# Relation passes of a graph network: three accumulators in turn in place of one

## The reference

```python
t = jnp.einsum('nd,rdo->rno', h, weight)
msg = t[etype, src]
agg = jax.ops.segment_sum(msg, dst, num_segments=h.shape[0])
return jax.nn.relu(agg + bias)
```

## Time and profile before

| | us |
|---|---|
| Median of 3 runs | 8612.98 |
| Lowest and highest of them | 8594.42, 8615.65 |
| Profiled execution: span from its first to its last instruction | 8619.9 |
| Busy in the span: POOL, PE, PEld, DVE, ACT | 5243.4, 4852.2, 2990.1, 3573.0, 1730.7 |
| Pass 1, from 4014 us on | about 1200 |
| Pass 3, from 7417 us on | about 1167 |

### The profile page before, as it was taken

One profiled execution on the slowest core, in us unless ns is written; L12 is line 12 of the kernel. 1 busy time (PEld: TensorE's weight loads), 2 busy tenths in 40 slices (PEclk: granted clock), 3 DMA queues, 4 the chain that ended last, 5 costly groups with the idle time before them and its releaser, 6 DMA issues. The chain is left out here.

```text
span 8619.9 us, 69117 instructions
## 1 busy us (share of the span) xinstructions
PE 4852.2 (56%) x17004; PEld 2990.1 (35%) x17004; DVE 3573.0 (41%) x9196; ACT 1730.7 (20%) x7055; POOL 5243.4 (61%) x5610
## 2 busy tenths in 40 slices
PE   3202235555557777777455543777777876655554
PEld 1100014444435555543333332222223663333332
DVE  4201014333335555564222224444445776244445
ACT  0000001111123333322000002222223874000000
POOL 5577756666666666632666662666665882366665
PEclk6655557777778888888666666878888998866666
DMA  3001012222235555554333335656666884333333
GB/s 96 2 3 39 15 40 90 90 89 89 91 116 176 177 175 175 177 114 156 92 93 93 92 93 67 186 184 187 187 187 177 267 271 156 117 93 92 91 94 85
DMA packets 422550, 1037.69 MB, mean 120 GB/s; under 512 B 159993, under 2 KB 188189, under 8 KB 415516
## 3 DMA queue, kind: packets, MB, share of 16 engines
q0 software_dynamic: 223616, 552.46, 22.9%
q1 hardware_dynamic: 198556, 480.95, 17.4%
HBM read 716.74 MB, written 316.30 MB: 120 GB/s over the span
## 5 line engine op out<-in xcount | busy, mean ns | idle before, releaser
L944 POOL DMA_INDIRECT rel_rows<-relation_rows,rel_ring_row x1640 | 1558.3, 950 | 1177.7 <-ACT rel_ring_end L937 695.1
L956 PE MATMUL rel_sums<-rel_rows,rel_hot 128*128 128x256 f32 x3280 | 1197.1, 509 | 1178.3 <-issue 448.5
L956 PEld LDWEIGHTS rel_sums<-rel_rows,rel_hot 128*128 128x128 f32 x3280 | 785.7, 252 | 1590.1 <-issue 1076.9
L982 DVE TENSOR_TENSOR g_acc<-rel_sums,g_acc 128x256 f32 x1224 | 517.8, 423 | 1532.9 <-DMA records_by_dst<-g_big 548.5
L1913 POOL DMA_INDIRECT nmax_rows<-messages,nmax_ring_row x832 | 788.6, 948 | 566.3 <-ACT nmax_ring_row L1869 327.6
L761 POOL DMA_INDIRECT rows_by_src<-spread_rows,spread_ring_place x832 | 803.2, 965 | 483.8 <-issue 254.3
L838 POOL DMA_INDIRECT both_rows<-batch_normed,both_ring_row x832 | 791.0, 951 | 460.9 <-ACT both_ring_end L807 231.3
L605 POOL DMA_INDIRECT records_by_dst<-sort_ring_rec,sort_ring_place x784 | 810.4, 1034 | 390.6 <-issue 241.2
L739 PE MATMUL spread_p_r<-g_big,spread_hot_t 128*128 x1664 | 631.5, 545 | 542.0 <-ACT spread_hot_t L674 358.8
L1961 DVE TENSOR_TENSOR g_big<-nmax_short,g_big 128x512 f32 x832 | 575.7, 692 | 659.9 <-PE nmax_short L1934 288.6
L1934 PE MATMUL nmax_short<-nmax_rows,g_ident_b 128*128 128x512 bf16 x2496 | 800.3, 436 | 0.0
(11 more groups left out here) (443 smaller groups left out, 6114.8 us busy)
## 6 DMA issues: line engine op xcount, KB each, us to landing
kept_rows<-nmax_rows SPq DMA_DIRECT2D x208, 536.0 KB
g_big<-kept_rows SPq DMA_DIRECT2D x208, 536.0 KB
both_out_rows<-rows_by_src SPq DMA_DIRECT2D x202, 520.0 KB
att_local_row<-local_of_edge SPq DMA_DIRECT2D x52, 512.0 KB
rel_rows<-relation_rows,rel_ring_row POOLq DMA_INDIRECT x1640
relation_rows<-mix_table SPq DMA_DIRECT2D x25, 1024.0 KB
relation_rows<-fin_table SPq DMA_DIRECT2D x25, 1024.0 KB, 3.9
rows_by_src<-spread_rows,spread_ring_place POOLq DMA_INDIRECT x832
```

The source lines that it names most:

```text
L944: pool.indirect_dma_start(rows[:, j, 0:words], None, table, bass.IndirectOffsetOnAxis(ap=ring_row[:, j:j + 1], axis=0)).then_inc(landed[n ...
L956: last = nc.tensor.matmul(sums[:, unit % slots, 0:width], hot[:, j, :], rows[:, j, :], start=of == 0, stop=of == GRAIN[k] - 1)
L982: nc.vector.tensor_tensor(at, sums[:, unit % slots, 0:width], at, ALU.add).then_inc(added, 1)
```

## The change

The sums go in turn to three accumulators: unit 0 to `acc`, unit 1 and 2 to two accumulators in `g.big`, unit 3 to `acc` again. An add waits for the add three back, the last one that wrote the same accumulator. ScalarE clears the two new ones, after it has staged the first eight groups; the second and third sum wait for that (`blank`). After the last sum, VectorE adds both into `acc`.

```diff
@@ aggregate
         sums = m.ps("sums", [P, slots, 8 * 512 // slots])
+        side = g.big[:, 0:2 * (T + 1) * width].rearrange("p (a t d) -> p a t d", a=2, d=width)
+        into = [acc[:, :, 0:width], side[:, 0], side[:, 1]]
+        blank, joined = m.sem("blank"), m.sem("joined")
@@ scalar
             for n in range(groups):
+                if n == ring:
+                    for s in range(2):
+                        nc.scalar.activation(side[:, s], g.iota[:, 0:1].unsqueeze(2).broadcast_to([P, T + 1, width]),
+                                             ACT.Copy, scale=0.0).then_inc(blank, 1)
                 if n >= ring:
                     act.wait_ge(summed, n - ring + 1)
@@ vector
-                    if unit:
-                        dve.wait_ge(added, unit)
-                    at = acc[:, bass.ds(tiles[unit % 16], 1), 0:width].rearrange("p t d -> p (t d)")
+                    if unit in (1, 2):
+                        dve.wait_ge(blank, unit)
+                    if unit >= 3:
+                        dve.wait_ge(added, unit - 2)
+                    at = into[unit % 3][:, bass.ds(tiles[unit % 16], 1), :].rearrange("p t d -> p (t d)")
                     nc.vector.tensor_tensor(at, sums[:, unit % slots, 0:width], at, ALU.add).then_inc(added, 1)
             dve.wait_ge(added, groups * per)
+            for s in range(2):
+                if s:
+                    dve.wait_ge(joined, 1)
+                nc.vector.tensor_tensor(into[0], into[0], side[:, s], ALU.add).then_inc(joined, 1)
+            dve.wait_ge(joined, 2)
```

## The result

| | before | changed |
|---|---|---|
| Median of 9 runs, us | 8607.44 | 8632.24 |
| Lowest and highest, us | 8594.42, 8615.65 | 8626.14, 8643.96 |
| Span of the profiled execution, us | 8619.9 | 8630.4 |

The changed kernel takes 1.0033 times as long, with a 95% interval of 1.0025 to 1.0042: slower by 28 us, or by 24.8 us if one goes by the medians. It lies at the bound of 0.3% that the prediction drew between no change and slower.

The account below looks back on a forecast made before the run. The prediction took GpSimd's gathers, one per 1.25 us plus stalls from late counts, to bound the two passes. From a median of 8612.98 us, joins +28.6, body -3 and tail -5 gave 8633 us, range 8598 to 8655.

Parts of the forecast that it names:

- the case with no credit: Rival, chance 0.30: late counts let the faster adds win nothing in body or tail; the joins stand alone, 8642 us.
- The 8 us of credits: Savings expected in pass 3 from the loosened waits: 3 us in the body and 5 us in the tail.
- Joins, +28.6: Two VectorE adds of 128x6656 after each pass's last sum, nothing beside them: 14.3 us per pass, 28.6 for both.
- Zeroing, 0: ScalarE's clearing of the two new accumulators, 5.7 us each, hidden behind VectorE's wait for the first gather: 0 us, 1 at most.
- Adds 0.34 us apart: VectorE's adds, waiting for the add three back, would start 0.34 us apart instead of 0.567.
- Body, -3: During pass 3, quicker adds might let TensorE get a group further before the next slow stretch: 3 us saved.
- The comparison of pass 1 with pass 3: Stalls per group, 0.69 us with two adds and 0.74 with four, taken to cap the body's gain at 10 us.
- a sign of being right: TensorE's waits for adds in pass 3 would be well under 408 us, with hardly any time won.
- Tail, -5: At the end of pass 3, quicker adds would let TensorE's last group start 3 us sooner: 5 us saved.
- The reading of the stalls: GpSimd's stalls, 143.5 and 149.6 us in passes 1 and 3, come from late completion counts, not the add chain.

Follow-up runs that it names:

- no_joins: The changed kernel without the two joins at the end of each pass, so two thirds of the sums are missing from the result: 8610.59 us, ratio 1.0000.
- two_accumulators: The changed kernel with one extra accumulator in place of two, each add waiting for the one two back, one join per pass: 8619.33 us, ratio 1.0012.
- old_waits: The changed kernel with the old condition, each add waiting for the add before; accumulators, zeroing and joins kept: 8633.23 us, ratio 1.0023 to the kernel before.
- paced_210: The kernel before with a GpSimd memset of 210 columns behind each gather of the relation passes: 8561.98 us against 8556.77, ratio 1.0005.

## Why the prediction was right, and where it was not

- *Time and range.* 8633 was forecast and 8632.24 measured, inside 8598 to 8655. Part of this is luck: the median of the kernel before is 8607.44 over nine runs and not 8612.98, which makes the step +24.8 us by medians or +28 by the ratio, where +20.6 was forecast. What came is the case with no credit, to which 0.30 was given, 28.6 us; no change had 0.57 and slower 0.33, and the measured ratio has its middle just past the bound. The 8 us of credits did not come, and the starting point had been 5.5 us too high; the two nearly cancel.
- *Joins, +28.6.* Right in size and place: 7.09 us each, 14.22 a pass, all on the path. Shown by `no_joins` (1.0000) and `two_accumulators` (1.0012, half of the loss).
- *Zeroing, 0.* Right: 5.74 us each where 5.7 was worked out, hidden by the wait for the first rows, in pass 3 by a quarter of a microsecond.
- *Adds 0.34 us apart.* Right: 0.33. But dropping the wait was worth nothing all the same, because the counts come late with slow adds and with fast ones. What the Trainium skill (VectorE: DVE Perf Modes, "The DRAIN you can't avoid") says of chaining without semaphores, that it saves nothing, does not hold for these adds: 0.567 us apart with a wait for the add before, 0.33 us with a wait three back.
- *Body, -3.* Wrong in size: 0. The comparison of pass 1 with pass 3 had pointed to it; I took the 0.05 us per group between them as something to gain, and it was not. Both passes run at 1.42 us per gather. TensorE's waits for adds were 408.0 us and are 431.4 us in `old_waits`. In the changed kernel they should have fallen well under 408 us, as a sign of being right; they rose to 464.3. That sign failed, and the rival with no credit had it right: TensorE waits as before. These are waits for late counts and not for slow adds, since 325.2 us are left even with the adds cut to 8 columns, and no such wait decides the end.
- *Tail, -5.* Not borne out. In the profiled executions the last sum of pass 3 ended 14.8 us behind the last gather before, and 13.4 us after: 1.4 us. `old_waits` has 19.0, `two_accumulators`, with the fast adds, 13.2, and `no_joins`, with them too, 15.2. These are single executions that differ by as much as the credit, and `no_joins` is no faster than the kernel before.
- *The reading of the stalls.* The prediction held that the counts come late and that this ends when GpSimd pauses. The runs bear that out: with a pace of 1.57 us, nothing is late any more. It took the stalls, though, for a loss that could in principle be won back. In these kernels they are none. They fill up the difference between issuing at 1.25 us and the 1.42 us per gather that a pass takes anyhow, and paid as memsets (`paced_210`) or as stalls they come to the same. What sets the 1.42 us is open.

## What to carry to other kernels

If a stretch keeps its length to a microsecond while its stalls change their number and place, don't look for the chain of waits that makes them: divide the length by the number of the busiest engine's items, and test that rate by making the engine slower. Then look whether the items themselves are late before you call the rate theirs: here the rows of a gather landed 2.4 us after its start all along. A shorter dependent chain on an engine that works a third of the time can earn at most what stands at the end of the stretch, so price its fixed costs there first; two whole-buffer adds behind a barrier cost their full 14 us. Waits of the trace that look large, 408 us of TensorE for VectorE's adds, can all be slack; cut the work that is named to a stub, and see whether the stretch gets shorter.

## What was not expected of the hardware

In every kernel of this study whose issue was no slower than that, a pass took 1.40 to 1.43 us per gather, with 128 rows of 1 KB, 128 rows of 512 bytes or 64 rows of 1 KB, and with rings of six or eight groups. The rows themselves landed 2.2 to 2.4 us after a gather's start (medians), late counts or not.

While GpSimd issued every 1.25 to 1.285 us, completions of TensorE, VectorE and GpSimd's own memsets came late by up to tens of us and then several at once (30.6 us for TensorE's group that ended at 7969.41 in the earlier trace rows). By the trace of pass 3, ScalarE staged a group over 2 us after TensorE had ended the one that it waited for in 74% of the groups of the kernel before, in 59% at 1.41 us per gather, and in none at 1.57. In none either at 1.41 us with half of TensorE's instructions. So both the gathers and TensorE's instructions bear on it. That lateness and the 1.42 us belong to one backlog is an inference: when the surplus of the issue goes, both the stalls and the lateness go.

What sets the 1.42 us was not found, nor whether it belongs to a gather or to a chunk with all that is done for it, nor why half of TensorE's instructions took up to 1% off it. Whether the recording of the executions takes part was not tested. A gather that carries two chunks at once was not tried.
